# Cached attention by batches: the value pages of a batch asked for in two halves, the second one a step later

## The chip, the cores and the metric

The kernel runs on one core of a Trainium2 chip (trn2). The metric is the device time of one execution in microseconds (us). Engines: PE is TensorE (its weight loads are shown apart as PEld), DVE is VectorE, ACT is ScalarE, POOL is GpSimd, and SP is SyncE, which here does little but issue transfers; "SPq" in a row is SP's own stream of instructions.

## The reference, cut to what matters

64 sequences of 32 tokens run through a cached attention, a second attention, a mix and a feed-forward layer. Only the cached attention is touched. Each sequence b has its own row of 16 page numbers in a table; every page holds 32 cached keys and values for 8 key heads of width 128:

```python
L = NPP * PSIZE                                    # 16 pages of 32 keys
kc = k_cache[block_table].reshape(bsz, L, HK, D)
vc = v_cache[block_table].reshape(bsz, L, HK, D)
k_all = jnp.concatenate([kc, k], axis=1)           # and the 32 own keys
v_all = jnp.concatenate([vc, v], axis=1)
scores = jnp.einsum('bqhd,bkhd->bhqk', q, k_all) * SCALE
scores = jnp.where(valid[:, None, None, :], scores, -1e+30)
probs = jax.nn.softmax(scores, axis=-1)
o = jnp.einsum('bhqk,bkhd->bqhd', probs, v_all)
```

32 query heads share 8 key heads. All of it is float32.

## The kernel before, in words

**Stages.** Stage 1 makes queries, own keys and own values and writes them to HBM. Stage 2 is the cached attention (`stage2`, lines 776 to 1064), written out for all 64 batches on PE, ACT and DVE, and run as loops over pairs or fours of batches on SP and POOL. Stage 3 (`over_heads`, line 1067) is the output projection, and stages 4 to 6 follow it. One queue of instructions per engine runs through stage 2 and on into stage 3.

**PE's order in stage 2** (lines 1054 to 1061). For each batch b: the scores of b, 8 groups (`scores`, L1033); then the values of the batch before, b - 1, two groups (`values`, L1050). After the loop come the values of batch 63, with no scores ahead of them. The first group of a batch's values waits for all 16 of its value pages (`v_loaded`, L1042), for its own values, for `o_copied` (L1044) and for the softmax of the batch. Its second group adds to `pv_done`, so `pv_done` is 2b when the values of batch b - 1 are done.

**The value pages.** `v_all` has two slots; batch b uses slot b % 2. A page is one transfer of 128 KB (128 rows of 1024 bytes) from `vpool`, issued by SP at L830. `load_v_pages` first reads 8 page numbers from the table into registers of SP (L826), then issues 8 transfers. `pair_of` (L837) waits for `pv_done` at 2b (L841), which says that the slot of batch b - 1 is free, and then asks for both halves of batch b + 1. PE needs these pages only after it has done the values of b and the scores of b + 2.

**The other queues.** POOL, for each batch: once the scores of b are done it asks for the queries and own keys of b + 2 (L70, L74) and gathers the key pages of b + 2 inside SBUF by 16 copies (L84); once `pv_done` is 2b it asks for the own values of b + 1 (L858); then it stores the output of b - 1 (L864). ACT makes the exponentials and the normalised weights (L902, L909) and copies the output out of PSUM (`copy_o`, L915). DVE makes the masked scores (L962) and transposes the weights (L980).

**The end of stage 2.** Behind SP's last value pages stand, in SP's queue, the first loads of stage 3: `load_w` (L1083, behind a wait at L1093 that is long met) and two `load_h` (L1088). ACT's order there is written out at lines 938 to 945: the last two normalises, then `first_w_high` for the four parts of the first weights of stage 3 (L1117 to L1123; it waits for that `load_w`), then `copy_o(62)`, then two `h_high`, then `copy_o(63)`. PE's values of batch 63 wait for `copy_o(62)` through `o_copied`.

Of the kernel before, what the change touches and what calls it, by code (L numbers as in the profile page):

```python
# [37 lines left out]
PAGES, PSIZE, NPP = 64, 32, 16  # L38
# [737 lines left out]
def stage2(nc, hold, c, a, scratch):  # L776

    with ExitStack() as opened:
# [10 lines left out]
        v_all = place(nc.sbuf_tensor("v_all", [P, 2, NPP + 1, 2 * D], F32))  # L789
# [30 lines left out]
        pool_passed = hold(nc.semaphore("pool_passed"))  # L820

        def sync(sp):
            def load_v_pages(b, slot, half):

                first = half * NPP // 2
                page = nc.values_load_multi_w_load_instructions(  # L826
                    c["table"][0:1, bass.ds(b * NPP + first, NPP // 2)], engines=(mybir.EngineType.SP,), min_val=0, max_val=PAGES - 1,
                    skip_runtime_bounds_check_because="the reference's indices lie in the pool")[1]
                for k in range(NPP // 2):
                    sp.dma_start(v_all[:, slot, first + k, :], a["vpool"][bass.ds(page[k], 1)].rearrange("o p n -> p (o n)")  # L830
                                 ).then_inc(v_loaded[slot], 16)

            for b in range(2):
                for half in range(2):
                    load_v_pages(b, b, half)

            def pair_of(i, first, last):  # L837
                for j in range(2):
                    b = i * 2 + j
                    if not (first and j == 0) and not (last and j == 1):  # L840
                        sp.wait_ge(pv_done, b * 2)  # L841
                        for half in range(2):
                            load_v_pages(b + 1, 1 - j, half)

            pair_of(0, True, False)
            with sp.Fori(1, LAST) as i:
                pair_of(i, False, False)
            pair_of(LAST, False, True)
# [169 lines left out]
        def tensor(pe):  # L1018
# [35 lines left out]
            for b in range(B):  # L1054
# [6 lines left out]
            values(GROUPS - 1)  # L1061

    return dict(sync=sync, gpsimd=gpsimd, scalar=scalar, vector=vector, tensor=tensor,
                k_gathered=k_gathered, o_store_free=o_store_free, shift_done=shift_done, o_copied=o_copied, pv_done=pv_done)

# [990 lines left out]
```

## Time and profile before

| | us |
|---|---|
| median of 3 runs | 3032.32 |
| lowest and highest run | 3031.26, 3038.28 |
| the profiled execution's own time | 3035.94 |
| its span, first to last instruction | 3034.4 |

The profile is of one execution. Its rows give the start and the busy time of instructions in us from the span's start, counts as "x16", and in square brackets the idle time ahead of a piece with what ended it. In rows of one source line the durations are in ns, followed by the starts of the first and the last of the instructions in us; a row on landing tells the us from the issue of a transfer to its arrival. In tables by stretch the columns are, for each engine, busy us and instructions, then the granted TensorE clock as a share of full speed, the busy share of the DMA engines and the GB/s they moved.

### The profile page before, as it was taken

How to read it: one execution, taken by the hardware profiler on the slowest of the kernel's cores; microseconds unless marked ns; L12 is line 12 of the kernel's file. 1: busy time of each engine (PE TensorE's matmuls, PEld its weight loads, DVE VectorE, ACT ScalarE, POOL GpSimd, SP SyncE). 2: the span in 40 equal slices, each digit the busy share in tenths (PEclk: the TensorE clock that was granted, in tenths of full speed). 3: DMA queues.
4: the chain of work that ended last, by engine and by line, in shares of the span. 5: the costliest groups of instructions: out<-in, count | busy, mean ns of one | idle time of the engine just before them, and what ended most of it. 6: DMA issues, size and time to landing. Idle time of an engine off the chain costs nothing.

```text
span 3034.4 us, 89812 instructions
## 1 busy us (share of the span) xinstructions
PE 2971.7 (98%) x36256; PEld 2364.6 (78%) x36256; DVE 1803.1 (59%) x3587; ACT 1545.8 (51%) x2885; POOL 592.5 (20%) x1398
## 2 busy tenths in 40 slices
PE   8999999999999999999999999999999999999999
PEld 7777778767777777777777888888888888888887
DVE  5777779477777777777875444432333333544545
ACT  6666655377777777777775122222333343322221
POOL 0000001355455455455541000000000000300000
PEclk9999999999999999999999999999999999999999
DMA  5333334566666666666767444322323332843311
GB/s 163 109 106 111 107 115 150 176 208 217 208 217 215 216 216 207 216 214 209 226 216 215 125 117 118 111 80 104 105 88 104 122 103 85 244 148 111 111 42 56
DMA packets 505622, 456.28 MB, mean 150 GB/s; under 512 B 32961, under 2 KB 469569, under 8 KB 500674
## 3 DMA queue, kind: packets, MB, share of 16 engines
q1 hardware_dynamic: 470402, 354.41, 38.4%
q0 software_dynamic: 34880, 96.85, 9.5%
q8 instruction: 273, 4.47, 0.6%
q14 instruction: 67, 0.55, 0.1%
HBM read 321.03 MB, written 130.02 MB: 149 GB/s over the span
## 4 chain that ended last, share of the span: by engine, by line
PE 78%; issue 2%; DVE 0%; ACT 0%; POOL 0%; DMA 0%; POOLq 0%; DVEq 0%; ACTq 0%
PE ps_o L1050 17%; PE ps_scores L1033 12%; PE s_ps L58 8%; PE s_ps L60 8%; PE s_ps L59 8%; PE s_ps_proj L58 5%; PE s_ps_proj L59 5%; PE s_ps_proj L60 5%; PE ps_o L1033 4%; PE s_ps_o L1574 1%; PE s_ps_scores L1550 1%; PE yv_ps L60 1%; PE yv_ps L59 1%; PE yv_ps L58 1%; PE s_ps L1749 0%
## 5 line engine op out<-in xcount | busy, mean ns | idle before, releaser
L1050 PE MATMUL ps_o<-weights_t,v_all 32*128 32x128 f32 x17408 | 524.1, 273 | 37.5 <-issue 37.2
L1050 PEld LDWEIGHTS ps_o<-weights_t,v_all 32*128 32x128 f32 x17408 | 504.6, 188 | 70.9 <-issue 70.3
L902 ACT ACTIVATE probs<-masked,shift 128x544 f32<-128x544 f32 x512 | 380.7, 743 | 126.5 <-DVE shift L962 119.3
L962 DVE CUSTOM_DVE_ANT_0 masked<-ps_scores,reach,scale_now 128x544 f32<-128x544 f32 x384 | 294.0, 766 | 241.8 <-PE ps_scores L1033 235.8
L1033 PE MATMUL ps_scores<-k_slot,q_slot 128*32 128x288 f32 (+1 forms) x6144 | 399.3, 396 | 9.5 <-PEq L98 5.1
L84 POOL COPY k_slot<-k_pool 128x256 f32 x1024 | 371.9, 424 | 21.2 <-issue 20.8
L1133 ACT ACTIVATE s_h_hi<-s_h_raw 128x2048 fp32r<-128x2048 f32 x64 | 122.8, 1919 | 488.1 <-PE s_ps L60 479.3
L909 ACT ACTIVATE probs<-probs,inv 128x544 f32<-128x544 f32 x512 | 351.6, 734 | 0.1
L980 DVE STREAM_TRANSPOSE weights_t<-probs 128x544 f32<-128x544 f32 x512 | 347.8, 716 | 0.0
L1033 PEld LDWEIGHTS ps_scores<-k_slot,q_slot 128*32 128x32 f32 x6144 | 199.4, 110 | 159.4 <-issue 13.1
L58 PE MATMUL s_ps_proj<-y_hi,s_w_hi 128*128 128x512 f32 x640 | 253.1, 395 | 0.0
L59 PE MATMUL s_ps_proj<-y_lo,s_w_hi 128*128 128x512 f32 x640 | 250.0, 391 | 0.0
L60 PE MATMUL s_ps_proj<-y_hi,s_w_lo 128*128 128x512 f32 x640 | 249.1, 389 | 0.0
L415 ACT ACTIVATE turning<-ps_proj 64x512 f32<-64x512 f32 x256 | 151.9, 593 | 139.9 <-PE ps_proj L60 138.4
L58 PE MATMUL ps_proj<-x_hi,w_hi 128*128 128x512 f32 x512 | 203.0, 396 | 0.0
L58 PE MATMUL s_ps<-s_w_hi,s_h_hi 128*128 128x512 f32 x512 | 199.5, 390 | 0.0
L60 PE MATMUL ps_proj<-x_hi,w_lo 128*128 128x512 f32 x512 | 199.4, 390 | 0.0
L59 PE MATMUL ps_proj<-x_lo,w_hi 128*128 128x512 f32 x512 | 199.3, 389 | 0.0
L58 PE MATMUL s_ps<-s_h_hi,s_w_hi 128*128 128x512 f32 x512 | 199.3, 389 | 0.0
L59 PE MATMUL s_ps<-s_w_lo,s_h_hi 128*128 128x512 f32 x512 | 199.2, 389 | 0.0
L60 PE MATMUL s_ps<-s_h_hi,s_w_lo 128*128 128x512 f32 x512 | 199.2, 389 | 0.0
L60 PE MATMUL s_ps<-s_w_hi,s_h_lo 128*128 128x512 f32 x512 | 199.2, 389 | 0.0
(205 smaller groups left out, 4940.8 us busy)
## 6 DMA issues: line engine op xcount, KB each, us to landing
v_all<-vpool_in SPq DMA_DIRECT2D x1024, 128.0 KB, 3.4
qT_scratch<-k_pool SPq DMA_DIRECT2D x32, 1024.0 KB, 5.1
q_slot<-qT_scratch POOLq DMA_DIRECT2D x64, 512.0 KB, 4.2
oT_scratch<-o_t POOLq DMA_DIRECT2D x64, 512.0 KB, 5.6
s_h_raw<-oT_scratch SPq DMA_DIRECT2D x32, 1024.0 KB, 5.7
aT_scratch<-s_o_t SPq DMA_DIRECT2D x32, 1024.0 KB, 5.7
s_h_raw<-aT_scratch SPq DMA_DIRECT2D x32, 1024.0 KB, 5.7
w_raw<-w_in SPq DMA_DIRECT2D x11, 1024.0 KB, 7.7
```

The costliest lines, as they stand in the source:

```text
L58: pe.matmul(out, a_hi, b_hi, start=start, stop=False)
L59: pe.matmul(out, a_hi, b_lo, start=False, stop=False)
L60: return pe.matmul(out, a_lo, b_hi, start=False, stop=stop)
L84: m = pool.tensor_copy(k_slots[slot][:, first + k, :], k_pool[:, bass.ds(page[k], 1), :].rearrange("p o n -> p (o n)"))
L415: act.activation(swapped[g][to, :], bank[g][of, :], ACT.Copy)
L902: act.activation(probs[:, n % BUF, :], masked[:, n % 2, :], ACT.Exp, bias=shift[:, n % BUF:n % BUF + 1], scale=-1.0, accum_out=total[:, n ...
L909: act.activation(probs[:, n % BUF, :], probs[:, n % BUF, :], ACT.Copy, scale=inv[:, n % BUF:n % BUF + 1]).then_inc(w_done, 1)
L962: dve.tensor_tensor_reduce(masked[:, n % 2, :], scores_place(n)[:, LOW:LOW + KEYS], reach[:, slot, :], scale_now[:, slot, k:k + 1], 3.0e38 ...
L980: dve.transpose(weights_t[:, grp % 4, n % G, :], probs[:, n % BUF, :]).then_inc(turned_w, 1)
L1033: m = pe.matmul(scores_place(n)[q * S:(q + 1) * S, cols], q_slots[j][:, head, r * S:(r + 1) * S], k_slots[j][:, pages, head * PSIZE:(head ...
L1050: m = pe.matmul(ps_o[:, q, e * GS:(e + 1) * GS], v_all[rows, j, t, e * D:(e + 1) * D], weights_t[rows, grp % 4, :, t * S:(t + 1) * S], sta ...
L1133: act.activation(h_hi[k % 2][:, :, :].rearrange("p g (b s) -> p b g s", s=S), h_raw[k % 2][:, :, :].rearrange("p b (g s) -> p b g s", s=S) ...
```

## The change

Reading page numbers becomes a function of its own, `pages_of`, and the issue of 8 transfers another, `load_v_pages`. Ahead of the loop only three halves are asked for: both of batch 0 and the first of batch 1. In the loop, for batch b: the page numbers of the second half of b are read ahead of the wait; after the wait for `pv_done` at 2b that second half is issued (slot b % 2), then the page numbers of the first half of b + 1 are read and that half is issued (slot of b + 1). For b = 63 only the second half of 63 is issued, behind a wait for `pv_done` at 126 that was not there before. PE, ACT, DVE and POOL, and the counts that they wait for, are as before.

```diff
-            def load_v_pages(b, slot, half):
+            def pages_of(b, half):
 
                 first = half * NPP // 2
-                page = nc.values_load_multi_w_load_instructions(
+                return nc.values_load_multi_w_load_instructions(
                     c["table"][0:1, bass.ds(b * NPP + first, NPP // 2)], engines=(mybir.EngineType.SP,), min_val=0, max_val=PAGES - 1,
                     skip_runtime_bounds_check_because="the reference's indices lie in the pool")[1]
+
+            def load_v_pages(page, slot, half):
                 for k in range(NPP // 2):
-                    sp.dma_start(v_all[:, slot, first + k, :], a["vpool"][bass.ds(page[k], 1)].rearrange("o p n -> p (o n)")
+                    sp.dma_start(v_all[:, slot, half * NPP // 2 + k, :], a["vpool"][bass.ds(page[k], 1)].rearrange("o p n -> p (o n)")
                                  ).then_inc(v_loaded[slot], 16)
 
-            for b in range(2):
-                for half in range(2):
-                    load_v_pages(b, b, half)
+            load_v_pages(pages_of(0, 0), 0, 0)
+            load_v_pages(pages_of(0, 1), 0, 1)
+            load_v_pages(pages_of(1, 0), 1, 0)
 
             def pair_of(i, first, last):
                 for j in range(2):
                     b = i * 2 + j
-                    if not (first and j == 0) and not (last and j == 1):
+                    if not (first and j == 0):
+                        page = pages_of(b, 1)
                         sp.wait_ge(pv_done, b * 2)
-                        for half in range(2):
-                            load_v_pages(b + 1, 1 - j, half)
+                        load_v_pages(page, j, 1)
+                        if not (last and j == 1):
+                            load_v_pages(pages_of(b + 1, 0), 1 - j, 0)
```

## Rows read from the trace of the kernel before

**Rows 1.** The page: busy time by engine, and the chain that ended last.
```profile
PE 2971.7 (98%) x36256; PEld 2364.6 (78%) x36256; DVE 1803.1 (59%) x3587; ACT 1545.8 (51%) x2885; POOL 592.5 (20%) x1398
...
PE 78%; issue 2%; DVE 0%; ACT 0%; POOL 0%; DMA 0%; POOLq 0%; DVEq 0%; ACTq 0%
```

**Rows 2.** Timeline of PE, one batch of stage 2: scores, then values.
```profile
1081.87 2.04 PE L1033 MATMUL ps_scores<-k_slot,q_slot 128*32 128x288 f32 x32
...
1089.34 7.87 PE L1050 MATMUL ps_o<-weights_t,v_all 32*128 32x128 f32 x272
1097.15 1.12 PE L1033 MATMUL ps_scores<-k_slot,q_slot 128*32 128x288 f32 x16
```

**Rows 3.** Waits of SP's queue in stage 2: us in total, times, longest.
```profile
SPq L826 <- PE ps_o L1050: 276.8, 62, 9.4
```

**Rows 4.** SP's queue: the reads of page numbers (L826), whole stage.
```profile
L826 SPq TENSOR_LOAD <-table x128: 521/527/1114, 598.3 to 1620.4; - x128
L826 SPq FUSED_REGOPS  x120: 51/58/77, 644.5 to 1605.1; - x120
```

**Rows 5.** SP's first read and first transfer behind two waits.
```profile
L826 SPq TENSOR_LOAD <-table x1: 522/522/522, 1113.7 to 1113.7; - x1
...
1114.43 3.40 SPq L830 DMA_DIRECT2D v_all<-vpool_in  x6
```

**Rows 6.** First halves of three batches: eight issues of L830, and their landing.
```profile
L830 SPq DMA_DIRECT2D v_all<-vpool_in x8: 333/416/975, 1082.8 to 1087.8; - x8
...
DMA to landing us min/median/max: 2.4/3.2/4.2
...
L830 SPq DMA_DIRECT2D v_all<-vpool_in x8: 327/333/823, 1114.4 to 1118.5; - x8
...
DMA to landing us min/median/max: 2.2/3.4/3.9
...
L830 SPq DMA_DIRECT2D v_all<-vpool_in x8: 333/333/1201, 1198.7 to 1203.2; - x8
...
DMA to landing us min/median/max: 2.1/3.1/3.8
```

**Rows 7.** Transfers into v_all over the whole stage.
```profile
L830 SPq DMA_DIRECT2D v_all<-vpool_in x1024: 327/333/1952, 599.2 to 1625.4; - x171
...
DMA to landing us min/median/max: 1.9/3.5/6.3
```

**Rows 8.** Timeline of PE over a slower batch.
```profile
1113.54 2.04 PE L1033 MATMUL ps_scores<-k_slot,q_slot 128*32 128x288 f32 x32
...
1121.01 3.84 PE L1050 MATMUL ps_o<-weights_t,v_all 32*128 32x128 f32 x125
1125.04 3.85 PE L1050 MATMUL ps_o<-weights_t,v_all 32*128 32x128 f32 x128 [0.19 <-issue]
1129.61 0.93 PE L1050 MATMUL ps_o<-weights_t,v_all 32*128 32x128 f32 x19 [0.72 <-issue]
```

**Rows 9.** PE's idle time from 620 to 1646: us in total, times, longest.
```profile
PE ps_o L1050 <- issue: 37.2, 34, 5.8
```

**Rows 10.** Timeline of POOL in one batch.
```profile
1114.36 0.71 POOL L858 DMA_DIRECT2D v_all<-v_pages_scratch  x1 [1.65 <-PE ps_o L1050]
1116.95 0.56 POOL L864 DMA_DIRECT2D oT_scratch<-o_t  x1 [1.88 <-issue]
1121.89 0.54 POOL L70 DMA_DIRECT2D q_slot<-qT_scratch  x1 [4.38 <-PE ps_scores L1033]
```

**Rows 11.** Timeline of all engines, the end of stage 2.
```profile
1622.12 7.96 PE L1050 MATMUL ps_o<-weights_t,v_all 32*128 32x128 f32 x272
...
1625.80 0.42 SPq L1083 DMA_DIRECT2D s_w_raw<-wo_in  x1
...
1632.62 2.19 ACT L1121 ACTIVATE s_w_hi<-s_w_raw 128x512 fp32r<-128x512 f32 x4 [2.50 <-DMA s_w_raw<-wo_in]
1634.71 1.00 ACT L915 ACTIVATE o_t<-ps_o 128x1024 f32<-128x1024 f32 x1
...
1635.92 10.33 PE L1050 MATMUL ps_o<-weights_t,v_all 32*128 32x128 f32 x272 [5.84 <-issue]
```

**Rows 12.** Stretches at the end of stage 2, with granted clock and DMA share.
```profile
1626.00:1636.00 10.00, 4.16 (x148) 4.00 (x141) 5.09 (x11) 7.21 (x15) 0.00 (x0) 0.90 1.05 304
1636.00:1641.00 5.00, 5.00 (x96) 5.00 (x100) 3.42 (x2) 3.53 (x2) 0.54 (x1) 0.51 1.06 323
```

## The prediction

> **What bounds the kernel now.** I read the page first. PE is busy 98% of the span and holds 78% of the chain that ended last; every other engine stands near 0% in the chain [rows 1]. So whatever makes PE stand still is paid in full, and whatever SP or POOL do is free until PE waits for it. The change touches only SP's queue, so there is one question: at which moment does PE come to the pages, and at which do they land?
>
> The timeline of PE gives the first half of the answer. Scores begin at 1081.87 and values at 1089.34, so the scores take 7.47 us; values take 7.81 (to 1097.15), together 15.28 us a batch [rows 2]. Call S the start of the scores, which is also the end of the values of an earlier batch and so the moment at which `pv_done` rises. The values of the next batch can start at S + 7.47, and no sooner. The waits of SP's queue say that SP waits for `pv_done` 62 times, 276.8 us in all, 4.5 us a batch [rows 3]: SP is never late now, and the pages that it asks for after S are needed a whole batch after the next values. No row shows PE waiting for a page.
>
> **Part 1: the read ahead of the wait.** One of the two reads leaves the path behind the wait. A read takes 0.527 us in the median with 0.058 of register work before it [rows 4], 0.6 together with the gap. In the row it begins at 1113.7, and the first transfer is issued at 1114.43, which is S + 0.89 with S = 1113.54 [rows 5, 8]. After the change the first transfer leaves at about S + 0.28. The read itself lands in SP's 4.5 us of waiting, which covers it; without that cover it would cost SP 0.6 us a batch, and PE nothing.
>
> **Part 2: the second half of b after the wait.** Before, these 8 transfers were issued one batch earlier. Now they start at S + 0.28 and PE wants all 16 pages at S + 7.47. From the first to the eighth issue the three batches of the rows take 5.0, 4.1 and 4.5 us [rows 6], and I use 4.6, since most issues take 0.33 but in each burst one or two are held up to 0.8 to 1.2 us. So the eighth leaves at S + 4.9. Landing takes 3.1 to 3.4 us in the median, and 3.8 to 4.2 for the slowest of each eight [rows 6]. The batch waits for the last increment of the last transfer. I take 3.8, the lowest of the three maxima, because the slowest need not be the eighth. The pages are whole at S + 8.7, which is 1.2 us after PE could begin. This happens for batches 1 to 62: 62 x 1.2 = **75 us**. The bounds: a landing as the medians have it (3.1) gives 0.5 us x 62 = 32 us; an eighth that takes as long as 4.5, between those maxima and the 6.3 of [rows 7], gives 1.9 x 62 = 118 us.
>
> Here a price of the Trainium skill speaks against my sum. The rows have landing at 2.1 to 2.4 us for the fastest, 3.1 to 3.4 in the median. The page "DMA: Bandwidth & Descriptors", section "Anatomy of one DMA — SWDGE (gpsimd) path", gives a fixed 2.0 us plus bytes over 436 GB/s, an estimate of 2.3 us for 128 KB; by that the second half would be whole at S + 7.2, and PE would not wait. The trace agrees for the fastest of each eight alone, since the queue is loaded while POOL's transfers run.
>
> **Part 3: the first half of b + 1.** It is read and issued behind those 8, that is until about S + 10, as the second burst is now, and PE needs it a batch later. It costs nothing; the cover is some 12 us. SP still has time left in a batch of 16 to 17 us. The bytes per batch are the same, and POOL's three transfers hang on PE as before [rows 10]. The 8 transfers that are missing ahead of the loop were hidden, and bring nothing.
>
> **Part 4: what PE gets back.** Inside the values PE stands still now and then with the reason "issue": 0.19 and 0.72 us in one batch [rows 8], 37.2 us in 34 times over the stage, of which 5.8 is the end of the stage [rows 9]. The pages of SP and the queries of POOL (at 1121.89) are in flight just then, so these stalls look like PE's own instructions coming late through busy DMA engines. If PE starts its values 1.2 us later while the transfers keep their place behind S, some of the overlap goes. Bounds: nothing, or all 31 us. I take a third, **-10 us**, as most of POOL's transfer still lies under the values.
>
> **Part 5: the end of the stage.** SP's last work before was over at 1625.7, and `load_w` left at 1625.80; ACT waited for it until 1632.62, then took 2.19 us for the weights and 1.00 for `copy_o(62)`, and PE began its last values at 1635.92, idle for 5.84 [rows 11]. Now SP waits until `pv_done` is 126, which PE reaches at the end of the values of 62, at 1630.1. Then come 8 issues (0.2 + 4.6 + 0.3, rounded), so `load_w` leaves at about 1635.1 instead of 1625.8, and everything behind it in ACT's queue is late by that: the weights, `copy_o(62)`, PE's last values. That is **+9 us**, once. The last pages themselves land at 1630.1 + 0.2 + 4.6 + 3.8 = 1638.7 and hide behind it. The two `load_h` move with it, beside PE. The last values take 10.33 us and not 7.8, at a granted clock of 0.51, the lower level of 1.2 GHz, after PE's idle time [rows 11, 12]; it idles longer now, so I keep that as it is, with +0 to +4 for the range.
>
> **Sum.** 75 - 10 + 9 = +74 us. Against the profiled execution's own 3035.94 that is 3110; that execution is 3.6 us above the median of the runs, so the median should be **3107**.
>
> **The rivals.**
> - *In time.* If the issues run at their steady pace and the eighth lands as the fastest do, the pages are whole by S + 7.5: 0.28 + 4.1 + 3.1. For it: the medians of landing, and a quieter start since the read is gone. Against it: all three maxima [rows 6]. Then only the end of the stage is paid, about 3032 + 9 = 3041, or a few us less with stalls given back.
> - *A slower queue.* The last increment comes as late as 4.5 us or more behind the eighth issue, from one DMA engine that is behind the others because of POOL's store of 512 KB [rows 10], and nothing is given back: 118 + 9 + 4 gives 3163.
> - *Faster.* The place is PE's instruction supply within the values. If moving PE against the transfers removes all 31 us of stalls and the pages are in time, the sum is -31 + 9 = -22: 3010. It decides only if the eighth lands within 2.6 us of its issue (7.47 - 0.28 - 4.6), which no maximum of the rows allows.
> - *It doesn't do what it says.* If SP were still at the pages of the batch before when `pv_done` rises, the read would not be ahead of anything. SP's 4.5 us of waiting [rows 3] speaks against it; it would add 0.6 us a batch, 37 us: 3144.
>
> **How the numbers follow.** My forecast, 1.2 us a batch with the end of the stage, has 0.60, and its own range from the bounds is about 3060 to 3150. The slower queue has 0.20, the read that is no gain 0.03, in time 0.12, faster 0.05. For 8 times in 10 the range reaches from 3055 (late by 0.5 us: 32 - 15 + 9, about 3058) to 3160. This kernel's measurement can tell about 0.3%, 9 us, from no change. In time lies at that edge, so I give half of it to "same": faster 0.05, same 0.06, slower 0.89.
>
> **What would show it.** In the profile after: SP's first transfer behind the wait at S + 0.3, with the read ahead of the wait; the distance from the start of scores to the start of values 8.7 and not 7.47 in nearly every batch, with PE waiting for v_all; `load_w` at about 1700 on the new clock, some 5 us behind the end of the values of batch 62, and PE idle about 15 us and not 5.84 before the last values. Stages 1 and 3 to 6 keep their lengths. It is wrong if the values start at S + 7.5 (part 2), if the stalls named "issue" go from 37 to near 0 or grow (part 4), or if ACT's wait for the weights is as short as now (part 5).

## The result and the profile after

The changed kernel takes **3187.22 us** (median of 4 runs, 3181.72 to 3190.06) against 3033.69 of the kernel before in the same comparison: a ratio of 1.0502, 95% interval 1.0482 to 1.0522. It is slower by 153.5 us. The prediction had the direction and the place, but forecast 74 us, and its range ended at 3160.

The page of the profile after; its lines answer to [rows 1]:

```profile
PE 3001.6 (94%) x36256; PEld 2388.2 (75%) x36256; DVE 1802.9 (57%) x3587; ACT 1546.0 (49%) x2885; POOL 591.4 (19%) x1398
...
PE 60%; DMA 9%; SPq 8%; issue 3%; DVE 0%; ACT 0%; DVEq 0%
PE ps_o L1054 17%; DMA v_all<-vpool_in 9%; SPq L832 8%; PE s_ps L58 8%; PE s_ps L60 8%; PE s_ps L59 8%; PE s_ps_proj L58 5%; PE s_ps_proj L59 5%; PE s_ps_proj L60 5%; PE s_ps_o L1578 1%; PE s_ps_scores L1554 1%; PE yv_ps L59 1%; PE yv_ps L6
```

PE's share of the chain has fallen from 78% to 60%. The pages (9%) and SP's issue of them (8%) have come in. PE's waits of the kernel after (us in total, times, longest), beside [rows 9], and SP's wait, beside [rows 3]:

```profile
PE ps_o L1054 <- DMA v_all<-vpool_in: 126.7, 62, 3.8
PE ps_o L1054 <- issue: 34.0, 27, 12.9
...
SPq L832 <- PE ps_o L1054: 433.3, 63, 14.4
```

The first row did not exist before. It has 62 waits, one for each batch from 1 to 62, 2.04 us in the mean. SP still waits for PE, 6.9 us a batch and not 4.5, so SP is not short of time: the transfers are merely asked for too late for their use.

The timeline of PE after, over two batches, beside [rows 2, 8]:

```profile
1102.73 9.50 PE L1054 MATMUL ps_o<-weights_t,v_all 32*128 32x128 f32 x272 [3.01 <-DMA v_all<-vpool_in]
1112.17 2.04 PE L1037 MATMUL ps_scores<-k_slot,q_slot 128*32 128x288 f32 x32
...
1121.17 5.84 PE L1054 MATMUL ps_o<-weights_t,v_all 32*128 32x128 f32 x195 [1.46 <-DMA v_all<-vpool_in]
```

The last two rows are one batch: its scores begin at S = 1112.17 and its values at S + 9.0. The first row has something else: values that take 9.50 us instead of 7.8. The table by stretch tells why (columns as in [rows 12]):

```profile
1099.70:1103.10 3.40, 0.39 (x16) 0.37 (x16) 3.40 (x10) 3.40 (x7) 2.29 (x5) 1.00 0.81 237
1103.10:1106.50 3.40, 3.40 (x76) 3.40 (x72) 2.79 (x7) 3.19 (x8) 3.40 (x11) 0.50 0.72 255
1106.50:1112.10 5.60, 5.60 (x204) 5.54 (x200) 0.00 (x0) 0.19 (x1) 1.23 (x4) 1.00 0.02 3
```

PE stood still for 3 us, and right behind that its granted clock is 0.50 for 3.4 us, the lower level of 1.2 GHz: 76 matmuls in that stretch against 204 in the 5.6 us that follow. The kernel after has 19 such falls between 630 and 1760 us, each beginning within 1.5 us of the end of a wait for pages of 1.8 to 3.8 us, while 42 of the 61 waits in that stretch are followed by none; the kernel before has no fall between 630 and 1614 us (granted clock 1.00 there).

SP's second half in that batch, and POOL's transfers beside it:

```profile
L832 SPq DMA_DIRECT2D v_all<-vpool_in x8: 332/333/1041, 1112.4 to 1116.9; - x8
...
DMA to landing us min/median/max: 2.0/3.9/4.3
```

```profile
1113.02 0.71 POOL L862 DMA_DIRECT2D v_all<-v_pages_scratch  x1 [5.28 <-PE ps_o L1054]
1114.03 0.56 POOL L868 DMA_DIRECT2D oT_scratch<-o_t  x1 [0.30 <-issue]
```

The first transfer leaves at S + 0.26, as said. The eighth leaves at S + 4.7, and the last of them is there 4.3 us later. Averaged over batches 3 to 60 from the starts and landings in the trace: first issue S + 0.26, eighth 4.84 us behind it, last landing 4.43 us behind that. That is S + 9.53, and the values start at S + 9.58.

The end of stage 2 after, beside [rows 11]:

```profile
1778.45 0.42 SPq L1087 DMA_DIRECT2D s_w_raw<-wo_in  x1
...
1783.85 2.19 ACT L1125 ACTIVATE s_w_hi<-s_w_raw 128x512 fp32r<-128x512 f32 x4 [14.21 <-DMA s_w_raw<-wo_in]
1785.94 1.00 ACT L919 ACTIVATE o_t<-ps_o 128x1024 f32<-128x1024 f32 x1
...
1787.15 8.64 PE L1054 MATMUL ps_o<-weights_t,v_all 32*128 32x128 f32 x206 [12.90 <-issue]
```

The chain is the predicted one: the last pages, `load_w`, ACT's four parts of the weights, `copy_o(62)`, PE. PE's idle time is 12.90 us and was 5.84.

**Where the time went** (spans: 3186.7 - 3034.4 = 152.3 us). Waits for pages 126.7. Values of batches 1 to 61: their times from the first matmul's start to the last one's, summed from the trace, exceed 7.6 us a batch by 64.7 us, and by 49.4 before, so +15.3. Within them the stalls, counted as steps of over 0.3 us from one matmul's start to the next, fell from 41.4 to 29.4 us, so the clock's falls cost about 15.3 + 12.0 = 27 us. From the first values of batch 62 to the end of stage 2: +9 us, of which 7 is the idle time. Together 151 us.

### The profile page after: what moved, and what is told of

Same layout as the page of the kernel before. It is cut to its first block, busy times and chain, and to the rows that moved or that the text cites. A ratio compares the mean times of both kernels' runs of the same rounds, so it can differ in the third digit from the quotient of the medians.

```text
span 3186.7 us, 89812 instructions
## 1 busy us (share of the span) xinstructions
PE 3001.6 (94%) x36256; PEld 2388.2 (75%) x36256; DVE 1802.9 (57%) x3587; ACT 1546.0 (49%) x2885; POOL 591.4 (19%) x1398
## 4 chain that ended last, share of the span: by engine, by line
PE 60%; DMA 9%; SPq 8%; issue 3%; DVE 0%; ACT 0%; DVEq 0%
PE ps_o L1054 17%; DMA v_all<-vpool_in 9%; SPq L832 8%; PE s_ps L58 8%; PE s_ps L60 8%; PE s_ps L59 8%; PE s_ps_proj L58 5%; PE s_ps_proj L59 5%; PE s_ps_proj L60 5%; PE s_ps_o L1578 1%; PE s_ps_scores L1554 1%; PE yv_ps L59 1%; PE yv_ps L60 1%; PE yv_ps L58 1%; PE s_ps L1753 0%
## 5 line engine op out<-in xcount | busy, mean ns | idle before, releaser
L1054 PE MATMUL ps_o<-weights_t,v_all 32*128 32x128 f32 x17408 | 552.0, 284 | 160.9 <-DMA v_all<-vpool_in 126.7
L1054 PEld LDWEIGHTS ps_o<-weights_t,v_all 32*128 32x128 f32 x17408 | 534.3, 198 | 196.9 <-DMA v_all<-vpool_in 156.6
L1037 PE MATMUL ps_scores<-k_slot,q_slot 128*32 128x288 f32 (+1 forms) x6144 | 391.9, 396 | 8.0 <-PEq L98 5.0
L59 PE MATMUL s_ps<-s_h_lo,s_w_hi 128*128 128x512 f32 x512 | 199.2, 389 | 0.0
```

The source lines that it names most:

```text
L59: pe.matmul(out, a_hi, b_lo, start=False, stop=False)
L1037: m = pe.matmul(scores_place(n)[q * S:(q + 1) * S, cols], q_slots[j][:, head, r * S:(r + 1) * S], k_slots[j][:, pages, head * PSIZE:(head ...
L1054: m = pe.matmul(ps_o[:, q, e * GS:(e + 1) * GS], v_all[rows, j, t, e * D:(e + 1) * D], weights_t[rows, grp % 4, :, t * S:(t + 1) * S], sta ...
```

## The experiments

All are compared with the kernel before on the same chip; ratios have their 95% interval. The edits are to the kernel after where nothing else is said.

**Three parts of the change, alone.** First, the read ahead without the moved half (edit to the kernel before):

```diff
                     if not (first and j == 0) and not (last and j == 1):
+                        page = pages_of(b + 1, 0)
                         sp.wait_ge(pv_done, b * 2)
-                        for half in range(2):
-                            load_v_pages(b + 1, 1 - j, half)
+                        load_v_pages(page, 1 - j, 0)
+                        load_v_pages(pages_of(b + 1, 1), 1 - j, 1)
```

> The order of the transfers of before, with the page numbers of the first half read ahead of the wait; the second half is not moved. Theory A (PE pays only because the second half is whole some 2 us after PE could start): the read ahead has no part in the loss, so 3034 us within 9 us, values start 7.5 us after the scores, no wait for v_all. Rival B (transfers that leave S + 0.14 instead of S + 0.8 meet POOL's two transfers in another way and slow everything down): longer landing and at least 20 us more, 3055 or above.

Measured: 3035.40 us, ratio 1.0006 (0.9996 to 1.0016). The read ahead is worth nothing in either direction; its cover is SP's waiting. Rival B of this run falls.

Then the end alone, in the order of before (edit to the kernel before, cut to the lines added for batch 63):

```diff
+                        page = pages_of(b, 1)
+                        sp.wait_ge(pv_done, b * 2)
+                        load_v_pages(page, j, 1)    # for b = 63 alone
```

> The order of before for all batches, only the second half of batch 63 is moved behind pv_done at 126. Theory A: PE's idle time ahead of its last values goes from 5.8 to about 13 us, so the kernel takes 7 us more, 3041 us. Rival: load_w is hidden in another way and the end costs nothing by itself, 3034 us; or it costs the 9 us and more that the prediction had, 3043 to 3047.

Measured: 3041.01 us, ratio 1.0028 (1.0015 to 1.0040), that is +7.5 us. By its interval that is 5 to 12 us, which agrees with the 9 us of the decomposition.

What is left of 153.5 us, some 146, is the second half of batches 1 to 62.

**The moment of asking.** The slot of the second half has been free for a whole batch, so the wait can be met earlier, after the first of the two value groups:

```diff
-                        sp.wait_ge(pv_done, b * 2)
+                        sp.wait_ge(pv_done, b * 2 - 1)
                         load_v_pages(page, j, 1)
                         if not (last and j == 1):
+                            sp.wait_ge(pv_done, b * 2)
                             load_v_pages(pages_of(b + 1, 0), 1 - j, 0)
```

> The kernel after, but the second half of b is asked for when the first of the two value groups of b - 1 is done (its slot has long been free), 3.8 us earlier; the first half of b + 1 waits as before. Theory A: the second half is whole at about S + 5.6, ahead of S + 7.5, so the whole wait and the clock's falls go; left is an end that is about 4 us longer than before: 3038 us. Rival B (splitting a burst of 16 transfers in two slows the queue): the time stays above 3100.

Measured: **3008.45 us**, ratio 0.9923 (0.9912 to 0.9935), 25 us faster than the kernel before. The second half is whole at S + 4.7 in the mean of batches 3 to 61. The waits of PE:

```profile
PE ps_o L1055 <- issue: 16.3, 17, 9.9
PE ps_o L1055 <- DMA v_all<-vpool_in: 0.5, 1, 0.5
```

Theory A had the wait gone, and it is (0.5 us), but it had 3038. The rest is in the first row: PE's stalls with the reason "issue" are 16.3 us, of which 9.9 is the end, where before they were 37.2 with 5.8 [rows 9]. So 31 us of stalls within the values became 6. I had this mechanism as the rival "faster" and gave it 0.05.

**The wait itself.** A count for each half, and PE begins with what it has:

```diff
-                    pe.wait_ge(v_loaded[j], b // 2 * 16 * NPP + 16 * NPP)
+                    pe.wait_ge(v_loaded[j][0], b // 2 * 8 * NPP + 8 * NPP)
...
                 for t in range(NPP + 1):
+                    if e == 0 and t == NPP // 2:
+                        pe.wait_ge(v_loaded[j][1], b // 2 * 8 * NPP + 8 * NPP)
```

> The kernel after, but with a count for each half: PE starts its values when the first half is there (asked for a batch before) and waits for the second half between page 7 and page 8, some 2 us later. Theory A: of the mean 2.05 us of lateness all but some 0.3 us is under the first 8 pages, so 127 us of waits fall to under 25 and the falls of the granted clock with them: 3040 to 3065 us. Rival C (the lost time is not in the waits but in the clock and PE's instruction supply, which fail whatever PE waits for): 3100 or above.

Measured: 3059.81 us, ratio 1.0089 (1.0073 to 1.0104).

```profile
PE ps_o L1056 <- issue: 41.3, 34, 14.1
PE ps_o L1056 <- DMA v_all<-vpool_in: 17.6, 23, 1.5
```

The waits fall from 126.7 to 17.6 us and the 19 clock falls to one. The stalls by "issue" stay as before (27 us without the end's 14.1). Against before the kernel pays 17.6 for waits and 8 for the end, 26 in all; the medians differ by 26.3. SP's order is that of the kernel after, so the loss is in PE's waiting and not in the order of the queue.

**What makes PE's instructions late.** The kernel before without the pages of batches 2 to 63, so with another output:

```diff
-                        for half in range(2):
-                            load_v_pages(b + 1, 1 - j, half)
+                        sp.sem_inc(pages_left_out, 1)
...
-                    pe.wait_ge(v_loaded[j], b // 2 * 16 * NPP + 16 * NPP)
+                    pe.wait_ge(v_loaded[j], 16 * NPP)
```

> The kernel before without the value pages of batches 2 to 63 (the batches use those of 0 and 1, so the output of the cached attention is another one). PE's order and waits are the same otherwise. Theory A (PE's stalls within the values are instructions that come late because SP's pages fill the DMA engines): the 49 us by which the values exceed 7.6 us a batch fall to under 10 and the end is 3 us shorter, about 2990 us. Rival B (these stalls are PE's own or come from POOL's transfers): they stay above 30 us, 3015 us or more.

Measured: 2990.62 us, ratio 0.9844 (0.9826 to 0.9862).

```profile
PE ps_o L1050 <- issue: 5.3, 7, 2.1
```

The excess of the values over 7.6 us a batch falls from 49.4 to 10.3 us. So most of PE's stalls within the values of the kernel before are made by SP's pages.

What comes late is PE's instructions. The profile names no releaser, but the packets in the traces show it. Between 630 and 1614 us the kernel before moves these packets of instructions:

```profile
q8 instruction: 190, 3.11, 1.3%
```

These are 190 packets of 16 KB, one for about every 256 instructions that PE runs there (24363 matmuls, 24358 weight loads and 183 waits for semaphores). The stalls come 382 or 383 matmuls apart, which with loads and waits is three times 256 instructions, or 1275, 1658 or 2041 apart, which is 10, 13 or 16 times 127.5 matmuls. All 33 stalls of over 0.15 us within the values lie at the same place of a block of 256, and each ends 1.2 to 1.6 us after such a packet is through. The packet of a block that stalls starts 2.2 us (median) after PE has passed the same place one block earlier; where nothing stalls, 1.1 us. The 25 stalls of the kernel after end 1.2 to 1.6 us behind a packet too, and the 4 that are left without SP's pages 1.3 to 1.5 us.

**Why the last increment comes 4.4 us after the eighth issue.** Two candidates: the eight transfers queued right behind, and POOL's own values and output store (128 and 512 KB), which leave at S + 0.9 and S + 2.0.

```diff
                         load_v_pages(page, j, 1)
+                        sp.wait_ge(v_loaded[j], i * 16 * NPP + 16 * NPP)
```

> The kernel after, but SP asks for the first half of b + 1 only when the second half of b has landed. Theory A1 (the eight transfers queued right behind make the last increment late, 4.4 us and not the 3.1 to 3.8 that I took): the wait of PE falls from 2.05 us a batch to 1.2 or less, 55 us and more off, 3130 us or below. Theory A2 (POOL's transfers or the pages themselves make it late): the wait stays within 0.3 us of 2.05; the time moves only by PE's stalls within the values, 3150 to 3220 us.

Measured: 3165.36 us, ratio 1.0396 (1.0360 to 1.0433).

```profile
PE ps_o L1055 <- DMA v_all<-vpool_in: 127.2, 62, 4.2
PE ps_o L1055 <- issue: 20.4, 13, 14.8
```

The wait is 127.2 us and was 126.7, with landing at 4.52 us after the eighth issue: A1 falls. The profiled execution is 16 us shorter than that of the kernel after (3172.1 and 3188.3). That is in the stalls by "issue", which go from 34.0 to 20.4, or without the end from 21 to 6. The granted clock falls about as often as in the kernel after (20 times from 630 to 1750 us).

```diff
                         pool.wait_ge(pv_done, b * 2)
+                        pool.wait_ge(v_loaded[j % 2], (i * 2 + j // 2) * 16 * NPP + 16 * NPP)
                         pool.sem_inc(pool_passed)
```

> The kernel after, but POOL asks for the own values and stores the output only when the second half of the pages has landed. Theory A2 (POOL's 640 KB behind S, which the pages share the DMA engines with, make them late): issues run near their steady 3.6 us and the last lands within 3 us, so the pages are whole by S + 7 and the wait goes: 127 us and the clock's 25 us off, 3040 us or below. Theory A1: the wait stays near 2 us a batch, 3150 us or above.

Measured: 3102.21 us, ratio 1.0189 (1.0155 to 1.0222). The eight issues of one batch with S = 1111.24, POOL's timeline, and PE's waits:

```profile
L832 SPq DMA_DIRECT2D v_all<-vpool_in x8: 332/333/498, 1111.5 to 1115.4; - x8
...
DMA to landing us min/median/max: 2.2/2.5/3.3
```

```profile
1103.90 0.72 POOL L862 DMA_DIRECT2D v_all<-v_pages_scratch  x1 [5.58 <-DMA v_all<-vpool_in]
1104.71 0.56 POOL L868 DMA_DIRECT2D oT_scratch<-o_t  x1
1105.48 0.74 POOL L70 DMA_DIRECT2D q_slot<-qT_scratch  x1 [0.21 <-issue]
```

```profile
PE ps_o L1055 <- issue: 68.4, 35, 12.6
PE ps_scores L1038 <- issue: 11.0, 10, 2.2
PE ps_o L1055 <- DMA v_all<-vpool_in: 6.8, 10, 2.0
```

Without POOL beside them the eight issues take 4.27 us (mean of batches 3 to 60; 4.84 after), and the last landing comes 2.77 us behind the eighth (4.43 after): the pages are whole 2.3 us sooner, and PE's waits for them are 6.8 us in all. A2 holds: POOL's transfers make the second half late. The time did not fall to 3040, because the cost moved. POOL's three large transfers now leave within 2 us, under the values, and PE's stalls by "issue" are 79 us where they were 34. Those within the values end 1.0 to 1.6 us behind a packet of instructions, as above. The granted clock still falls 13 times between 630 and 1680 us, 11 times behind a stall by "issue" of 2.0 to 4.0 us and once behind a wait for pages.

**The end of the fast version.** Batch 63 gets both halves at once again:

```diff
-                    if not (first and j == 0):
+                    if not (first and j == 0) and not (last and j == 1):
...
+                        if last:
+                            load_v_pages(pages_of(b + 1, 1), 1 - j, 1)
```

> The run with the second half one value group earlier took 3008 us; here batch 63 gets both halves at once as before, so that load_w is not held back. PE's idle time ahead of its last values goes from 9.9 back to about 6 us: 3004 us, 0.97 % below before. If that end is hidden behind something else, 3008 us.

Measured: 3008.06 us, ratio 0.9903 (0.9886 to 0.9920). It can't be told from the version without this edit (0.9912 to 0.9935): my 3004 was a miss, and the second value that I named, 3008, is what came. By the trace PE's gap ahead of its last values went only from 9.9 to 7.9 us.

**Another size.** 12 pages early and 4 late:

```diff
+        EARLY = 12
...
-                first = half * NPP // 2
+                first = half * EARLY
...
-                for k in range(NPP // 2):
+                for k in range(NPP - EARLY if half else EARLY):
```

> The kernel after with another size: 12 pages of a batch are asked for a batch early and only the last 4 behind the wait for pv_done at 2b. Theory A: from S the four issues and the 4.4 us of landing take some 6.5 us, inside the 7.5 us of scores, so no wait is left; the rest is as before, with an end some 5 us longer: 3025 to 3045 us. Rival (what is asked for behind S lands only with the last byte of POOL's store, at about S + 9 however few pages there are): PE still waits some 1.5 us a batch, 3120 us or above.

Measured: 3055.96 us, ratio 1.0065 (1.0045 to 1.0084).

```profile
PE ps_o L1055 <- issue: 48.7, 38, 10.8
PE ps_o L1055 <- DMA v_all<-vpool_in: 9.3, 12, 1.7
```

Waits fall from 126.7 to 9.3 us, so fewer late pages do land earlier, and the rival with one landing time for all sizes falls. Some batches still wait, and PE's stalls in the values rise (38 us without the end, 31 before), which is why it is 11 us above the range that I expected.

**The clock.** 20 matmuls, which the trace counts as 40, as it counts two for every float32 matmul of the values (272 for 136), fill the wait:

```diff
+                    if 1 <= b <= 60:
+                        for k in range(20):
+                            q = k % SEQ
+                            pe.matmul(ps_o[q * S:(q + 1) * S, 2 + k % 2, 2 * GS:2 * GS + LOW], c["ident"][:, 0:S], c["key_f"][:, 0:LOW], start=True, stop=True)
                     pe.wait_ge(v_loaded[j], b // 2 * 16 * NPP + 16 * NPP)
```

> The kernel after with 20 more matmuls (128x32 by 128x224, into unused columns) in each of the batches 1 to 60 between PE's scores and its wait for the pages, some 1.9 us of work that fills the wait and changes no result. Theory A (the fall of the granted clock, 19 stretches of 3.4 us in stage 2, follows from PE standing still, and costs about 27 us): the falls go, the pages land at the same moment, and the kernel with more work is faster, 3155 to 3170 us. Rival (the clock falls for another reason, or the fall costs nothing): 3187 us or more, with as many falls.

Measured: 3178.65 us, ratio 1.0476 (1.0456 to 1.0496). Stage 2 in one stretch, this kernel and the kernel after:

```profile
630.00:1745.00 1115.00, 1071.51 (x26876) 810.53 (x26872) 755.11 (x2087) 768.57 (x1532) 491.78 (x1203) 1.00 0.61 190
```

```profile
630.00:1760.00 1130.00, 985.15 (x24504) 756.94 (x24500) 754.32 (x2087) 769.15 (x1533) 492.38 (x1204) 0.97 0.60 188
```

```profile
PE ps_o L1058 <- DMA v_all<-vpool_in: 15.8, 24, 1.8
```

The 19 falls are gone (1.00 against 0.97), and PE's remaining waits for pages are 1.8 us at most. So the falls follow from PE standing still. The gain is smaller than the 17 to 32 us I expected. By the ratios (1.0476 and 1.0502) it is about 8 us, and the intervals of the two comparisons overlap, so it is not shown that this kernel is faster than the kernel after, only that the added matmuls cost no time. The traces tell what the clock took: the values' excess over 7.6 us a batch, less the stalls within them, is 64.7 - 29.4 = 35.3 us in the kernel after, 45.3 - 35.6 = 9.7 here, and 49.4 - 41.4 = 8.0 in the kernel before. So some 26 us go with the falls, near the 27 of the decomposition. Against them stand 6 us more of stalls in the values, which the wait had reduced, values that start some 0.1 us later in each batch, and 3 us more at the end of the stage.

**The end once more.** To the version of 3008 us, the first load of stage 3's weights ahead of SP's last wait:

```diff
+                        if last and j == 1:
+                            first_w(sp)          # wait for k_gathered, then load_w(sp, 0, 0)
                         sp.wait_ge(pv_done, b * 2 - 1)
```

> The run with the second half one value group earlier (3008 us), and in addition the first load of the weights of stage 3 is issued ahead of SP's wait for the last pages instead of behind it. Theory A (PE's idle 10 us ahead of its last values is the chain load_w, weights, copy_o): the idle time falls under 5 us and the kernel takes 3000 us within 4. Rival (the DMA engines or the softmax of the last batch hold PE there anyway): 3006 us or more.

Measured: 3004.18 us, ratio **0.9901** (0.9884 to 0.9917), at the upper edge of the 3000 within 4 that I expected.

```profile
1590.36 6.53 PE L1057 MATMUL ps_o<-weights_t,v_all 32*128 32x128 f32 x223
1591.70 0.34 SPq L1090 DMA_DIRECT2D s_w_raw<-wo_in  x1
1598.35 1.71 PE L1057 MATMUL ps_o<-weights_t,v_all 32*128 32x128 f32 x49 [1.46 <-issue]
1602.47 7.71 PE L1057 MATMUL ps_o<-weights_t,v_all 32*128 32x128 f32 x206 [2.42 <-DMA v_all<-vpool_in]
```

`load_w` is issued under the values of batch 62, and PE idles 2.42 us ahead of its last values instead of 9.9, now for the last pages. This is the lowest median of a whole kernel here, 1.0% below the kernel before. Whether it beats the version without this edit can't be said: their intervals overlap.

## Why the prediction was wrong

**Part 1** (the read, nothing): right, first issue at S + 0.26, and 3035.4 us with the read alone.

**Part 2** (75 us) is the step that failed, in its sizes. The mechanism was the right one: 62 waits, all for the second half. But the wait was 2.04 us a batch and not 1.2, which is 127 us. I took 3.8 us for the landing of the last increment, "the lowest of the three maxima"; it is 4.43. And I took 4.6 us for the eight issues; they take 4.84. With only 1.2 us between 8.7 and 7.47, an error of 0.85 in 8.7 makes the term 1.7 times as large. In the trace of before the eighth transfer is followed at once by eight others that add to the same count, so the landings of [rows 6] can be too short. The sixteenth has nothing behind it. In that trace it lands 4.55 us after its issue (mean of batches 3 to 60), the eighth by its record after 3.17 us. The 4.55 was the number to use, and with it the term is 1.96 x 62 = 122 us. That the late part lies beside POOL's two transfers was in the rows [rows 10], and I used it only for a rival. With POOL's transfers held back the last landing comes after 2.77 us.

**A term that was missing**: the granted clock. I looked at it at the end of the stage [rows 12], where 5.8 us of idle time had brought it down, and did not ask what 62 waits would do. The sum put it at nothing, and it cost about 27 us.

**Part 3** (nothing): no row of after has PE waiting for a first half.

**Part 4** (-10 us): -12 us by the stalls between PE's matmuls (41.4 to 29.4), so the size was right; the third had no row behind it, and that it fitted is in part luck.

**Part 5** (+9 us): right in its chain, +7.5 us alone.

So 75 - 10 + 9 became 127 + 27 - 12 + 9 = 151. Of the rivals, "a slower queue" had the landing right (4.5 us, 118 us) and POOL's transfers as its cause, and reached 3163; that one DMA engine was behind the others is not shown, and the clock is what carried the time past it. "In time" is refuted by the 62 waits. There the price of the Trainium skill, 2.0 us plus the bytes over 436 GB/s ("DMA: Bandwidth & Descriptors", "Anatomy of one DMA — SWDGE (gpsimd) path"), an estimate of 2.3 us from a fit for transfers that GpSimd issues and not SP, is near the fastest of the eight in the rows of the kernel after (2.0 us) and the median with POOL held back (2.5), and far below the slowest in the kernel after (4.3). "It doesn't do what it says" is refuted by SP's 6.9 us of waiting. "Faster" did not come about here, yet its mechanism exists: with the same halves asked for 3.8 us sooner, PE's stalls in the values fell from 31 to 6 us.

## What to carry to other kernels

When a load is moved nearer to its use, cost the arrival of its last byte, among the transfers that will be in flight there, and not the median landing of one. Where the margin is small, take the upper bound, and count with falls of the clock behind waits that stop PE for some 2 to 4 us (here 19 in 61 waits). A load that may be moved should be hung on the moment at which its buffer comes free and on what else is in flight, and not on an existing wait: here one value group earlier was the difference between 5.0% slower and 0.8% faster.

## What was not expected of the hardware

- Waits of 2 us in the mean (3.8 at most), once a batch, brought PE's granted clock from 1.00 to 0.50 in 19 stretches of 3.4 us; with some 2 us of matmuls in each wait (2.08 us in the batch at 1109.34 of that run), and no more than 1.8 us of waiting left, there was none.
- The transfers of two queues meet: SP's eight pages land 2.77 us behind the last issue without POOL's two transfers beside them and 4.43 us with them, and SP's issues themselves are slower then (4.27 and 4.84 us for eight).
- PE's stalls by "issue" depend on which transfers lie under a dense run of small matmuls: 37.2 us before, 5.3 without SP's pages, 79.4 with POOL's transfers moved under the values. Within the values each of them ends 1.0 to 1.6 us after a 16 KB packet of PE's instructions is through. Why holding SP's next half back also took them from 21 to 6 us, though those pages still leave under the values, stays open.
